# Three rounded products in the combine, with operands split two batches ahead by three engines

## What is computed

```python
x = _layernorm(x, norm_g, norm_b)
logits = jnp.einsum('bnd,esd->bnes', x, se)
dispatch = jax.nn.softmax(logits, axis=1)
combine = jax.nn.softmax(logits.reshape(x.shape[0], x.shape[1], -1), axis=-1)
slots = jnp.einsum('bnd,bnes->besd', x, dispatch)
gate = jax.nn.gelu(jnp.einsum('besd,edf->besf', slots, Wg) + bg, approximate=False)
up = jnp.einsum('besd,edf->besf', slots, Wu) + bu
eout = jnp.einsum('besf,efo->beso', gate * up, Wd) + bd
return jnp.einsum('bns,bso->bno', combine, eout)
```

## Time and profile before

| | us |
|---|---|
| median of three runs | 1206.83 |
| the profiled execution | 1211.8 |
| its span | 1210.1 |
| TensorE busy in the span | 1150.8 |
| VectorE | 781.7 |
| ScalarE | 663.5 |
| GpSimd | 581.5 |
| granted clock of TensorE, mean | 0.98 |

### The profile page before, as it was taken

One profiled execution on the slowest core, in us unless ns is written; L12 is line 12 of the kernel. 1 busy time (PEld: TensorE's weight loads), 2 busy tenths in 40 slices (PEclk: granted clock), 3 DMA queues, 4 the chain that ended last, 5 costly groups with the idle time before them and its releaser, 6 DMA issues.

```text
span 1210.1 us, 19118 instructions
## 1 busy us (share of the span) xinstructions
PE 1150.8 (95%) x6870; PEld 907.4 (75%) x6870; DVE 781.7 (65%) x1250; ACT 663.5 (55%) x946; POOL 581.5 (48%) x400
## 2 busy tenths in 40 slices
PE   6689999999999999999799999979999999999996
PEld 5466766666666666666688888867888888889885
DVE  5878797978787888764666777744544545522444
ACT  2545556565656565647778777755555555530112
POOL 6446655565656565512666666664445444440000
PEclk9889999999999999989899999998999999999998
DMA  4536454554546464640144335366654455364761
GB/s 134 126 87 154 96 135 106 144 138 122 149 115 152 110 154 99 177 123 1 53 157 157 123 122 183 105 173 228 183 174 146 155 165 180 113 213 149 244 232 53
DMA packets 126670, 170.29 MB, mean 141 GB/s; under 512 B 47041, under 2 KB 77186, under 8 KB 126594
## 3 DMA queue, kind: packets, MB, share of 16 engines
q1 hardware_dynamic: 124498, 168.74, 48.4%
q10 hardware_dynamic: 2096, 0.56, 0.2%
HBM read 72.26 MB, written 37.75 MB: 91 GB/s over the span
## 4 chain that ended last, share of the span: by engine, by line
PE 86%; DVE 4%; ACT 4%; issue 1%; SPq 1%; DMA 1%; POOL 1%; ACTq 0%; DVEq 0%; POOLq 0%
PE ring L437 12%; PE ring L438 11%; PE ring L439 11%; PE ring L1584 7%; PE ring L1419 6%; PE tail L1445 6%; PE ring L1434 5%; PE tail L437 4%; PE tail L438 4%; PE tail L439 4%; PE tail L1405 2%; PE ring L1467 2%; PE tail L1584 2%; PE ring L1421 2%; ACT pt L848 2%; ACT stg L833 2%
## 5 line engine op out<-in xcount | busy, mean ns | idle before, releaser
L1137 DVE TENSOR_REDUCE mx<-ring 128x4 f32<-128x512 f32 (+2 forms) x192 | 199.6, 1042 | 75.1 <-PE ring L1421 74.4
L848 ACT ACTIVATE pt<-ring 128x1024 f32<-128x1024 f32 (+1 forms) x192 | 167.2, 881 | 97.0 <-PE ring L1434 97.0
L705 POOL TENSOR_SCALAR_AFFINE_SELECT pt<-pt 128x512 f32<-128x512 f32 x128 | 82.0, 641 | 203.7 <-ACT pt L848 203.6
L1419 PE MATMUL ring<-qks 96*128 96x384 f32 (+3 forms) x512 | 139.1, 360 | 12.0 <-DMA qks<-stg 5.1
L1434 PE MATMUL ring<-qks 98*128 98x256 f32 (+3 forms) x512 | 138.8, 375 | 3.1 <-DVE mx L1137 1.7
L722 POOL TENSOR_TENSOR dl<-e,dh 128x1024 fp32r<-128x1024 f32 x32 | 76.6, 2404 | 94.6 <-ACT e L919 94.6
L746 POOL TENSOR_TENSOR hl<-hid,hh 128x512 fp32r<-128x512 f32 x64 | 82.6, 1301 | 77.2 <-ACT hh L954 77.2
L1419 PEld LDWEIGHTS ring<-qks 96*128 96x128 f32 x512 | 89.6, 196 | 30.9 <-ACT pt L848 18.9
L799 ACT ACTIVATE lat<-ring,blat 128x512 f32<-128x512 f32 x64 | 40.5, 683 | 121.7 <-PE ring L439 119.1
L1434 PEld LDWEIGHTS ring<-qks 98*128 98x128 f32 x512 | 81.4, 193 | 32.9 <-issue 19.8
L1255 DVE SCALAR_TENSOR_TENSOR hid<-ring,bias_e,gate 128x512 f32<-128x512 f32 x64 | 47.9, 748 | 81.1 <-ACT gate L948 49.6
(11 more groups left out here) (241 smaller groups left out, 3094.2 us busy)
## 6 DMA issues: line engine op xcount, KB each, us to landing
qks<-stg SPq DMA_DIRECT2D x384, 128.0 KB, 2.4
c_dram<-c2s SPq DMA_DIRECT2D x32, 512.0 KB, 5.0
c<-c_dram SPq DMA_DIRECT2D x32, 512.0 KB, 6.1
sl_dram<-sls SPq DMA_DIRECT2D x32, 256.0 KB, 3.4
wg<-in_wg SPq DMA_DIRECT2D x16, 512.0 KB, 5.5
wu<-in_wu SPq DMA_DIRECT2D x16, 512.0 KB, 6.3
wd<-in_wd SPq DMA_DIRECT2D x16, 512.0 KB, 6.9
sl<-sl_dram SPq DMA_DIRECT2D x16, 512.0 KB, 4.4
```

The source lines that it names most:

```text
L705: nc.gpsimd.affine_select(out=m, in_=m, compare_op=ALU.is_ge, fill=0.0, base=0, pattern=[[0, GH], [1, P]], channel_multiplier=-1).then_inc ...
L848: nc.scalar.activation(pt[j][:, h:h + heads, 0:n], heads_of(tile, heads, n), ACT.Exp, scale=SCALE).then_inc(empty, 1)
L1137: nc.vector.tensor_reduce(out=mx[:, g, h:h + heads, i], in_=heads_of(tile, heads, (i + 1) * P), axis=AX.X, op=ALU.max).then_inc(empty, 1)
L1419: nc.tensor.matmul(scores[:, h, :], qks[0:KS_ROWS, g, 0, h0 + h, i * P:(i + 1) * P], qks[0:KS_ROWS, g, 1, h0 + h, 0:n], start=(h == k), st ...
```

## The change

The combine is made of three fp32r products too. For each batch b ScalarE makes high parts of c2 (`c2h`, four tiles of two blocks, `combine_high`) and of eo (`eoh`, in parts of 4, 3 and 1 blocks, `eo_split`). The low parts of c2 are written over c2 itself (`c2l`): GpSimd does the first three pairs, VectorE the fourth (`combine_low`). VectorE makes eo's low part (`eol`, `eo_rest`). New buffers lie on tiles that the experts don't need any more. Work on batch b + 2 stands in turn b. The loops are written out, `apart` is gone from `clink`, and block 7 of batch 0 moves behind three blocks of batch 1.

```diff
 # sync, vector, scalar, tensor: Fori loops over q written out; example SyncE
-            repeat(sp, combine_two, B // 2 - 1)
+            for q in range(B // 2 - 1):
+                combine_two(q)
 # gpsimd
+            def combine_low(b, k):
+                i, ns = b % 2, slice(2 * k, 2 * k + 2)
+                pool.wait_ge(c2_high, 4 * b + k + 1)
+                nc.gpsimd.tensor_tensor(out=c2l[i][:, ns, :], in0=c2[i][:, ns, :], in1=fp(c2h[i][k][:, :, :]), op=ALU.subtract).then_inc(c2_low_pool, 1)
...
                 for f in range(NF):
+                    if not more and f in (0, 2):
+                        for k in ((0,), (1, 2))[f // 2]:
+                            combine_low(0, k)
...
+            for b in range(1, B):
+                for k in range(3):
+                    combine_low(b, k)
 # scalar
+            def combine_high(b, k):
+                i = b % 2
+                act.wait_ge(c2_loaded[i][k], (b // 2 + 1) * 16)
...
+                nc.scalar.activation(c2h[i][k][:, :, :], c2[i][:, 2 * k:2 * k + 2, :], ACT.Copy).then_inc(c2_high, 1)
+            def eo_split(b, part):
+                i, ns = b % 2, slice(EO_PARTS[part][0], EO_PARTS[part][-1] + 1)
...
+                else:
+                    act.wait_ge(acc_filled[i], b // 2)
+                nc.scalar.activation(eoh[i][:, ns, :], eo[:, ns, b, :], ACT.Copy).then_inc(eo_high[i], 1)
...
+            for b in range(B - 2):
+                for k in range(3):
+                    combine_high(b + 2, k)
+                for part in range(len(EO_PARTS)):
+                    eo_split(b + 2, part)
+                combine_high(b + 2, 3)
+                scale(b // 2, b % 2)
 # vector
+            def combine_low(b):
+                i = b % 2
+                dve.wait_ge(c2_high, 4 * b + 4)
+                nc.vector.tensor_tensor(out=c2l[i][:, 6:8, :], in0=c2[i][:, 6:8, :], in1=fp(c2h[i][3][:, :, :]), op=ALU.subtract).then_inc(c2_low_dve, 1)
+            def eo_rest(b, part):
+                i, ns = b % 2, slice(EO_PARTS[part][0], EO_PARTS[part][-1] + 1)
+                dve.wait_ge(eo_high[i], eo_count(b, part))
...
+                nc.vector.tensor_tensor(out=eol[i][:, ns, :], in0=eo[:, ns, b, :], in1=fp(eoh[i][:, ns, :]), op=ALU.subtract).then_inc(eo_low[i], 1)
...
                     dve.wait_ge(dve_chain, CHAIN + (b + part) * COMBINE_CHAIN + chain[0])
-                    apart(dve)
...
+            for b in range(B - 2):
+                norm_out(b // 2, b % 2)
+                for part in range(len(EO_PARTS)):
+                    eo_rest(b + 2, part)
+                combine_low(b + 2)
 # tensor
-                    if n % 2 == 0:
-                        pe.wait_ge(c2_loaded[i][n // 2], (q + 1) * 16)
+                    k = n // 2
+                    if k < 3:
+                        pe.wait_ge(c2_low_pool, 3 * b + k + 1)
+                    else:
+                        pe.wait_ge(c2_low_dve, b + 1)
+                    for part, ns in enumerate(EO_PARTS):
+                        if n in ns:
+                            pe.wait_ge(eo_low[i], eo_count(b, part))
                     for t in tiles:
-                        last = nc.tensor.matmul(acc[i][t // 2][:, t % 2, 0:DO], c2[i][:, n, t * P:(t + 1) * P], eo[:, n, b, :],
-                                                start=(n == 0), stop=(n == NS - 1))
+                        cols = slice(t * P, (t + 1) * P)
+                        last = mm3(acc[i][t // 2][:, t % 2, 0:DO], c2h[i][k][:, n % 2, cols], c2l[i][:, n, cols], eoh[i][:, n, :], eol[i][:, n, :],
+                                   n == 0, n == NS - 1)
...
             combine(0, 0, range(EARLY))
             pe.wait_ge(gu_drained[gu_slot(1, 2)], gu_count(NP - 1, 1, 2))
             down_step(NP - 1, 1, last_down)
-            combine(0, 0, range(EARLY, NS))
+            combine(0, 0, range(EARLY, NS - 1))
             pe.wait_ge(gu_drained[gu_slot(1, 3)], gu_count(NP - 1, 1, 3))
             pe.wait_ge(down_drained, E)
-            combine(0, 1)
+            combine(0, 1, range(EARLY))
+            combine(0, 0, range(NS - 1, NS))
+            combine(0, 1, range(EARLY, NS))
```

More of the change, by code:

```diff
@@ L322, in block_kernel @@
     c2 = [place(f"c2{i}", [P, NS, T], f32, raw_at[i]) for i in range(2)]
+    c2l = [place(f"c2l{i}", [P, NS, T], f32r, raw_at[i]) for i in range(2)]
+    set1_at = attn_at + 92 * KB
+    high_at = [[x_at, x_at + 4 * KB, x_at + 8 * KB, attn_at + 80 * KB], [set1_at + 4 * k * KB for k in range(4)]]
+    c2h = [[place(f"c2h{i}_{k}", [P, 2, T], f32r, high_at[i][k]) for k in range(4)] for i in range(2)]
+    eoh = [place(f"eoh{i}", [P, NS, DO], f32r, (attn_at + 60 * KB, attn_at + 68 * KB)[i]) for i in range(2)]
+    eol = [place(f"eol{i}", [P, NS, DO], f32r, (attn_at + 52 * KB, hidden_at + 8 * KB)[i]) for i in range(2)]
     y3 = [place(f"y3{i}", [P, NT, C], f32, hidden_at + i * 4 * KB) for i in range(2)]
@@ L376, in block_kernel @@
     c2_used = sem("c2_used")
+    c2_high, c2_low_pool, c2_low_dve = sem("c2_high"), sem("c2_low_pool"), sem("c2_low_dve")
+    eo_high, eo_low = [sem(f"eo_high{i}") for i in range(2)], [sem(f"eo_low{i}") for i in range(2)]
     acc_filled, acc_drained = [sem(f"acc_filled{i}") for i in range(2)], [sem(f"acc_drained{i}") for i in range(2)]
@@ L433, in block_kernel, with eo_count @@
     HALVES = (range(0, NT // 2), range(NT // 2, NT))
+    EO_PARTS = (range(0, 4), range(4, 7), range(7, 8))
+    def eo_count(b, part):
+        return b // 2 * len(EO_PARTS) + part + 1
     def mm3(dst, lh, ll, rh, rl, first, last):
@@ L954, in hid_split @@
                 nc.scalar.activation(hh[:, f, :], hid[f % 2][:, :], ACT.Copy).then_inc(hid_high, 1)
+            def combine_high(b, k):
+                i = b % 2
+                act.wait_ge(c2_loaded[i][k], (b // 2 + 1) * 16)
+                if (b, k) == (0, 0):
+                    act.wait_ge(w_low, 3 * E)
+                    act.wait_ge(w_low_pool, E)
+                elif (b, k) == (1, 0):
+                    act.wait_ge(gu_filled[gu_slot(1, 3)], gu_count(NP - 1, 1, 3))
+                nc.scalar.activation(c2h[i][k][:, :, :], c2[i][:, 2 * k:2 * k + 2, :], ACT.Copy).then_inc(c2_high, 1)
+            def eo_split(b, part):
+                i, ns = b % 2, slice(EO_PARTS[part][0], EO_PARTS[part][-1] + 1)
+                if b < 2:
+                    for k in range(2):
+                        act.wait_ge(eo_placed[k], (EO_PARTS[part][-1] + 1) * 32)
+                    if (b, part) == (0, 0):
+                        act.wait_ge(gu_filled[gu_slot(0, 3)], gu_count(NP - 1, 0, 3))
+                    elif (b, part) == (1, 0):
+                        act.wait_ge(down_filled, E)
+                else:
+                    act.wait_ge(acc_filled[i], b // 2)
+                nc.scalar.activation(eoh[i][:, ns, :], eo[:, ns, b, :], ACT.Copy).then_inc(eo_high[i], 1)
             def expert(p, i, more):
@@ L959, in expert @@
                     split_high(p + i, 1 - i, 0)
+                else:
+                    combine_high(0, 0)
                 gelu(p, i, 1)
@@ L963, in expert @@
                     split_high(p + i, 1 - i, 2)
+                else:
+                    eo_split(0, 0)
+                    combine_high(0, 1)
                 hid_split(p, i, 0)
+                if not more:
+                    combine_high(0, 2)
                 gelu(p, i, 2)
@@ L971, in expert @@
                     split_high(p + i, 1 - i, 3)
+                else:
+                    eo_split(0, 1)
+                    combine_high(0, 3)
                 gelu(p, i, 3)
@@ L989, in scale @@
                 last.then_inc(out_ready, 1)
[L991 to L995, removed]
+            for k in range(3):
+                combine_high(1, k)
+            for part in range(2):
+                eo_split(1, part)
+            eo_split(0, 2)
+            combine_high(1, 3)
+            eo_split(1, 2)
+            for b in range(B - 2):
+                for k in range(3):
+                    combine_high(b + 2, k)
[3 more added lines that the diff above has]
+                scale(b // 2, b % 2)
             scale(B // 2 - 1, 0)
@@ L1277, in expert @@
                     drain_down(p - 1, 1)
+                if not more:
+                    eo_rest(0, 0)
                 hidden(p, i, 2)
@@ L1280, in expert @@
                     split_low(p + i, 1 - i, 3)
+                else:
+                    eo_rest(0, 1)
                 hidden(p, i, 3)
+                if not more:
+                    combine_low(0)
             def pair(p):
@@ L1322, in norm_out @@
                 assert chain[0] == COMBINE_CHAIN, chain[0]
[L1324 to L1328, removed]
+            for part in range(2):
+                eo_rest(1, part)
+            eo_rest(0, 2)
+            combine_low(1)
+            eo_rest(1, 2)
+            for b in range(B - 2):
[3 more added lines that the diff above has]
+                combine_low(b + 2)
             norm_out(B // 2 - 1, 0)
```

(11 more changed lines are left out.)

8 lines of the change are left out of this document (3 added, 5 removed).

## The result

The changed kernel takes 1219.73 us in the median of six runs (1217.37 to 1220.47), the kernel before 1206.19 in six runs beside it (1203.87 to 1211.97). The ratio is 1.0108 with a 95% interval of 1.0089 to 1.0127: slower by 13.5 us, where a time of 1221 was forecast.

A forecast was written before the change was run, and what follows sets the result against it. It took TensorE's combine matmuls, 13.8 us a batch, as the bound. First scaling done at 1120.7, four turns of 16.3 and 38.2 to the end gave 1224.1, +14.0 on the span; added to 1206.83, 1221 us, range 1206 to 1229.

The forecast's parts named there:

- TensorE's part: Combine matmuls: three rounded products take 11.5 us a batch instead of 13.8, so TensorE could give back 18.4 us.
- Step 1: Last expert: GpSimd's added subtractions delay the down step; TensorE stands 4.4 us and loses 2.0 us to half clock.
- Step 2: Combine: store, loads, six roundings and scaling form a loop without TensorE, 14.9 us a turn with waits.
- Step 3: Combine: VectorE and GpSimd stop one another over a shared port, making turns 16.3 us on average.
- The two kinds of turn: Combine: VectorE's chain is through in time, 14.9 us, or its last steps follow GpSimd's third operation, 18.2 us.
- Step 4: Whole span: first scaling, four turns of 16.3 us and the end add up to 14.0 us more than before.
- R(0): End of batch 0's scaling in the combine, forecast at 1120.7 us.
- 0.9 (caught once, in part): Batch 0 of the combine: 0.9 us added before the first scaling's end for VectorE being held up once by GpSimd.
- R(4): End of batch 4's scaling in the combine, forecast at 1185.9 us, with 38.2 us from there to the end.
- The port hardly matters: Rival: in the combine VectorE and GpSimd miss each other and only the load loop is left; 1209 us, chance 0.18.
- The change does what it says: Rival: TensorE sets the combine's pace at 11.5 us a batch; 1190 us, chance 0.11.
- The low clock: Rival: TensorE stays at 1.2 GHz in the combine, 23.0 us a batch; 1262 us, chance 0.04.

The follow-up runs named there:

- e3: Changed kernel with stores issued by ScalarE and GpSimd's subtractions cut to 8 of 512 columns from batch 1 on: 1193.8 us.
- e4: Changed kernel with two of GpSimd's batch 0 subtractions behind the fourth hl and two early TensorE blocks instead of three: 1212.9 us.
- e1: Changed kernel with GpSimd subtracting 8 of 512 columns from batch 1 on, TensorE reading the high part again there: 1210.2 us.
- e2: Changed kernel with output stores issued by ScalarE behind its scaling instead of by SyncE: 1201.5 us.
- e8: Changed kernel with stores by ScalarE, two start subtractions later, two early blocks, and VectorE doing all subtractions from batch 1 on: 1198.7 us.
- e6: Changed kernel with stores by ScalarE, two start subtractions later, two early blocks, GpSimd and VectorE subtracting two pairs each from batch 1: 1189.2 us.

## Why the prediction was right, step by step

- **TensorE's part.** Right, and shown by e3: at 11.6 us a batch TensorE is busy throughout. In after, its 18.4 us of gain are gone into 18.6 us of waiting for `eol`, and more is lost at lower clock. Its busy share from 1140 to 1200 is 76%, within the 70 to 80% foretold.
- **Step 1, the start.** GpSimd was through 8.8 us behind the mark (forecast 8.7), TensorE stood for 4.1 (4.4), and batch 0 was full at 28.6 (28.0), where before had 19.7. GpSimd's two added subtractions took 6.4 us for 5.0 alone (forecast 6.2). For the clock, 23 matmuls took 5.05 us where 23 x 0.12 = 2.8, so 2.3 us (2.0). e4 takes 6.5 us of it back.
- **Step 2, the loop.** Right in kind and size: turns of 15.0, 14.8 and 15.5 for 14.9, and 15.2 in the mean of e1, where nothing else is left. e2 takes the store out, and the loop is gone.
- **Step 3, the port.** The two kinds of turn are there, with 17.4 for the 18.2 of the second: GpSimd's third operation ended 14.5 behind R(1) (14.8), and the rest of the chain took 0.8 (1.3). The mean of the first four turns is 16.2 (16.3). That it comes so close is in part luck, since 16.3 was the middle of a range and a little more, and not worked out from how often each kind comes. e1 and e8 show GpSimd to be the cause. One thing was wrong in it: I counted two-input steps only. The trace of after has L1083, one input, at 2.33 us against a median of 0.17, and it is the step that held up the first scaling. Its line by min/median/max ns, then VectorE in time:

```profile
L1083 DVE TENSOR_SCALAR r<-v x9: 168/170/2335, 1107.6 to 1209.7; 128x4 int32<-128x4 int32 x7, 128x2 int32<-128x2 int32 x2
```

```profile
1107.27 0.26 DVE L1078 TENSOR_SCALAR v<-mv 128x4 f32<-128x4 f32 x1
1107.56 2.33 DVE L1083 TENSOR_SCALAR r<-v 128x4 int32<-128x4 int32 x1
```

The Trainium skill, "SBUF — State Buffer", section "Who interferes with whom", says that `copy`, `cast` and `tensor_scalar` can go into a mode that takes both ports and then contend with GpSimd too. These rows agree as far as they go (they show the hold-up, not the mode), and e8, without GpSimd, has the same step at 0.17 throughout. I had drawn only on the rule for two inputs.

- **Step 4, the sum.** R(0) came 39.0 behind the mark, forecast 37.0: batch 0 was full 0.6 later, and the term "0.9 (caught once, in part)" was 2.3. R(4) came 103.6 (102.2), and from there to the end it took 37.0 (38.2). The total is 140.6 against 140.4: errors of +2.0, -0.6 and -1.2 that cancel. In time it is 1219.7 for 1221.
- **The rivals.** "The port hardly matters" gave 1209, and e1, which makes it true, measured 1210.2. "The change does what it says" (1190) is what e3 and e6 come near with 1193.8 and 1189.2; it wanted the loop gone and few catches left. The low clock didn't come to stay. From 1120 to 1200 the stretches of 10 us show 0.68 and 0.71 where TensorE waited, and 0.94 to 1.00 in between. But it came back with each long stop, as step 1 had it for later stops: behind those of 2.4 and 6.2 us the matmuls start 0.21 apart at first, behind those of 1.4 and 0.5 us they don't.

## What to carry to other kernels

When work is moved off the busiest engine onto others, add up each queue of the new helpers per turn, stops by one another included, and follow every wait once around: the gain of 0.07 us a matmul was real, and a store ahead of a load in one queue cost nearly all of it (17.4 of 18.4 us in the profiles). Put stores on another queue than the loads that a later turn waits for, and split work between VectorE and GpSimd so that GpSimd's operations lie beside VectorE's statistics or PSUM reads, not beside its small steps. With three edits (stores by ScalarE, two subtractions later in the start, two pairs each) the change that was 1.1% slower is 1.3% faster than before (e6).

## What the runs showed that I had not expected

- Two of VectorE's one-input steps from SBUF to SBUF, the `tensor_scalar` of L1078 and L1083, are held up by GpSimd as the two-input ones are: 2.33 us for 0.17 (L1083). `bn_stats`, also with one input, isn't: 407 to 429 ns in all 32 of the combine of after, those of batch 0 (from 1105.42) beside GpSimd. In e2 the four of a turn take 1.41 us beside GpSimd and away from it. The line of after:

```profile
L1397 DVE BATCH_NORM_STATS2 st<-y x32: 407/410/429, 1105.4 to 1208.8; 128x6 f32<-128x256 f32 x32
```

- A loop of three engines locks itself into one pattern: in e2 five turns in a row are 12.86 to 12.87 us, with the same two steps caught each time.
- The part that all these kernels share ends, in their profiles, between 1074.3 and 1078.6 us, and in that of before at 1083.7. One profile against another can thus be off by more than the effect; counting from a common event inside the program takes it out.
